# The first cross-attention's context made in the front of the self-attention, four lasting SBUF regions

## What is computed

```python
# 0: decoder block, 16 heads of 16; enc is the context
x = x + causal_attention(ln(x) @ qkv_w + qkv_b) @ proj_w + proj_b
k, v = enc @ k_w + k_b, enc @ v_w + v_b              # "context" of the first chain
x = x + attention(ln(x) @ q_w + q_b, k, v) @ out_w + out_b
x = x + gelu(ln(x) @ mlp1_w + mlp1_b) @ mlp2_w + mlp2_b
# 1: gated state update routed over tokens
tok = ctx @ W_proj + b_proj                            # "context" of the first chain, too
routed = softmax(x @ tok.T / 16) @ tok
x = ln((1 - u) * x + u * tanh(concat(r * ln(x), ln(routed)) @ W_n + b_n))
# 2: self-attention with 16 heads of 64, cross-attention over the context, gated feed-forward
# 3: cross-attention with 8 heads of 256 over the context, then ln
```

## Time and profile before

| | us |
|---|---|
| median of 3 runs | 2376.32 (2376.06 to 2378.35) |
| the profiled execution | 2376.05 |
| its span on the core | 2374.3 |

### The profile page before, as it was taken

The page is one execution under the profiler, slowest core; times in us unless marked ns, Lnnn a source line. Parts: engine busy times, 40 slices in busy tenths (PEclk is TensorE's granted clock), DMA queues, the critical chain, the costliest instruction groups (busy, mean ns, idle before and its releaser), DMA issues. The chain is left out here.

```text
span 2374.3 us, 27271 instructions
## 1 busy us (share of the span) xinstructions
PE 2087.5 (88%) x10510; PEld 1202.8 (51%) x10550; DVE 1119.0 (47%) x2012; ACT 932.2 (39%) x1435; POOL 776.8 (33%) x508
## 2 busy tenths in 40 slices
PE   3789998487979767999999999999998989898987
PEld 1444444275757554433343335334433857676766
DVE  5377662435252435455535554555450143535343
ACT  2246666133323222555545553554455322122211
POOL 3211100013032120566646664666466010202011
PEclk8899999799989887999999999999999989898989
DMA  5822420400000004000000000000000510000000
GB/s 115 131 39 38 51 29 2 113 1 0 1 0 0 1 1 122 1 1 1 1 1 1 1 1 1 1 1 2 1 2 1 161 28 1 9 1 9 0 9 9
DMA packets 48266, 52.77 MB, mean 22 GB/s; under 512 B 14730, under 2 KB 39052, under 8 KB 47732
## 3 DMA queue, kind: packets, MB, share of 16 engines
q1 hardware_dynamic: 48148, 51.17, 10.3%
HBM read 41.31 MB, written 8.80 MB: 21 GB/s over the span
## 5 line engine op out<-in xcount | busy, mean ns | idle before, releaser
L1734 POOL TENSOR_TENSOR total<-total,pr 128x1024 f32<-128x1024 f32 x192 | 464.9, 2421 | 241.9 <-ACT pr L1875 229.0
L1875 ACT ACTIVATE pr<-sc 128x1024 f32<-128x1024 f32 x256 | 259.7, 1021 | 355.6 <-PE sc L1654 355.6
L1755 DVE TENSOR_REDUCE pmax<-ring 128x1 f32<-128x512 f32 x512 | 325.8, 684 | 133.9 <-PE ring L1621 126.9
L1672 PE MATMUL o<-pr,v_pair 128*64 128x512 f32 x1024 | 275.7, 617 | 1.2
L1654 PE MATMUL sc<-q_full,k_full 64*128 64x512 f32 x1024 | 267.1, 591 | 0.0
L522 ACT ACTIVATE probs<-s 128x512 f32<-128x512 f32 (+1 forms) x304 | 163.2, 575 | 102.3 <-PE s L309 55.7
L1621 PE MATMUL ring<-k_round,q_round 64*128 64x512 f32 x512 | 185.0, 598 | 5.2 <-DVE pmax L1755 4.3
L1030 POOL TENSOR_TENSOR c_scores<-c_scores,c_total 128x1024 f32<-128x1024 f32 (+1 forms) x48 | 77.0, 1614 | 338.3 <-DVE c_total L986 338.3
L1621 PEld LDWEIGHTS ring<-k_round,q_round 64*128 64x128 f32 x512 | 74.4, 188 | 155.2 <-DVE pmax L1755 97.2
L394 DVE TENSOR_REDUCE row_max<-s 128x1 f32<-128x640 f32 (+3 forms) x128 | 127.3, 1020 | 47.4 <-PE s L291 47.1
L1672 PEld LDWEIGHTS o<-pr,v_pair 128*64 128x64 f32 x1024 | 51.2, 134 | 144.2 <-issue 142.4
(11 more groups left out here) (286 smaller groups left out, 3421.9 us busy)
## 6 DMA issues: line engine op xcount, KB each, us to landing
qk_dram<-qk_parts SPq DMA_DIRECT2D x32, 192.0 KB, 3.0
q_stack<-qk_dram SPq DMA_DIRECT2D x48, 128.0 KB
k_stack<-qk_dram SPq DMA_DIRECT2D x48, 128.0 KB
x<-in_x SPq DMA_DIRECT2D x4, 512.0 KB, 7.5
mlp_w<-in_L_xattn_mlp_w SPq DMA_DIRECT2D x2, 1024.0 KB, 8.3
wq<-in_L_xattn_Wq SPq DMA_DIRECT2D x2, 1024.0 KB, 6.5
wo<-in_L_xattn_Wo SPq DMA_DIRECT2D x2, 1024.0 KB, 14.9
hT<-in_L_xattn_ff_w SPq DMA_DIRECT2D x1, 2048.0 KB, 19.0
```

What stands on the lines that cost most here:

```text
L1672: ins = te.matmul(o[64 * j:64 * j + 64], v[n % 2][:, kt, 64 * j:64 * j + 64], probs[(U * n + u) % KEPT][:, j], start=kt == 0, stop=kt == T ...
L1734: pool.tensor_tensor(out=total[half][:], in0=other[:], in1=probs[at % KEPT][:], op=ALU.add).then_inc(sums, 1)
L1755: dve.tensor_reduce(part_max[:, j, t, half:half + 1], ring[i % RING][:], AX.X, ALU.max).then_inc(s1_free, 1)
L1875: act.activation(probs[here % KEPT][:], s2[at % 2][:], ACT.Exp).then_inc(s2_free, 1)
```

## The change

- The context work moves into `part_attention0`. Ten loads follow the projection's weights on SyncE. TensorE transposes the context before front unit 10, and multiplies after unit 12 and before `tops(0)`, with four more small matmuls for the values' bias. ScalarE keeps the results (it also scales `q_b` and writes `vcol`, which VectorE did), and `tops(0)` waits for it. GpSimd clears `vcol` behind `v_all`.
- The projection's bias is added to `x` by GpSimd in four pieces between head groups 1 to 4, in place of VectorE's one instruction.
- The 20 small loads of the chain are issued after head group 6 and awaited at the end of `part_attention0`; the five large ones (3.5 MB) are issued in `part_project0` and awaited by TensorE alone, inside the chain's first block.
- `bias0` and `kbd` are made by VectorE in `part_project0`. `part_context0` is gone.
- `ff2_w` of the last chain is loaded at the start of `part_chain2`, and TensorE waits for it at its first use.
- Four SBUF regions last through the program and are used in turn under many names. The first attention's scratch lies in `probs` and `qkv_w`.

```diff
-        raw, inverse = sb("raw", [P, 512]), sb("inverse", [P, 4, 4])
+        inverse = sb("inverse", [P, 4, 4])
...
-        h, hT = e.sa, sb("hT", [P, KC, B * T])
+        h, hT = e.sa, e.hT0
         qkv_w, qkv_b = sb("qkv_w", [P, KC, 3 * C]), sb("qkv_b", [P, 4])
-        rest = [sb(f"qk_rest{i}", [P, 512]) for i in range(RING)]
+        raw = qkv_w[:, 0, 0:512]
+        flat = [t[:].rearrange("p j n -> p (j n)") for t in probs[1:4]]
+        rest = [flat[0][:, 512 * i:512 * i + 512] for i in range(RING)]
         parts = [sb(f"qk_parts{i}", [P, 3, 512], BF16) for i in range(RING)]
+        k_w, v_w, t_w = (flat[2][0:96, 512 * i:512 * i + 512].rearrange("p (k c) -> p k c", k=2) for i in range(3))
+        ctx_rows = flat[1][:, 0:CC]
+        v_brep, t_brep = flat[1][0:S2, 256:512], flat[1][0:S2, 512:768]
+        tri, tri_bf = sb("tri", [P, P]), sb("tri_bf", [P, P], BF16)
+        k_b, t_b, q_b = sb("k_b", [P, KC]), sb("t_b", [P, KC]), sb("q_b", [P, KC])
...
+        CONTEXT, TURNED_AT = 10, 10
...
+            context_loads = [
+                (ctx_rows, lambda r: A["ctx_768"].rearrange("b s c -> (b s) c")),
+                (k_w, lambda r: r("L0_xattn_k_w")), (k_b[:], lambda r: column(A["L0_xattn_k_b"], KC)),
+                (v_w, lambda r: r("L0_xattn_v_w")), (v_brep, lambda r: A["L0_xattn_v_b"].partition_broadcast(S2)),
+                (t_w, lambda r: r("L1_xattn_W_proj")), (t_b[:], lambda r: column(A["L1_xattn_b_proj"], KC)),
+                (t_brep, lambda r: A["L1_xattn_b_proj"].partition_broadcast(S2)),
+                (q_b[:], lambda r: column(A["L0_xattn_q_b"], KC)),
+                (e.mask8[:], lambda r: A["mask_BxS2_bf0"].rearrange("b s -> (b s)").partition_broadcast(P)
+                 .rearrange("p (b s) -> p b s", b=B))]
+            assert len(context_loads) == CONTEXT
...
+            rows96 = lambda n: A[n].rearrange("(k p) c -> p k c", p=96)
+            for dst, src in context_loads:
+                sp.dma_start(dst, src(rows96)).then_inc(ctx_in, 16)
...
+                if n == G - 2:
+                    for dst, src in small:
+                        sp.dma_start(dst, src).then_inc(e.small_in, 16)
+            sp.wait_ge(e.small_in, 16 * len(small))
...
+                    pool.memset(e.vcol[:], 0.0).then_inc(power_set, 1)
...
+                if n <= 4:
+                    if n == 1:
+                        pool.wait_ge(e.proj_in, 48)
+                        pool.wait_ge(h_made, TILES // 2)
+                    pool.wait_ge(rows_cleared, n)
+                    x = e.x[:, 4 * n - 4:4 * n, :]
+                    pool.tensor_tensor(out=x, in0=x, in1=e.proj_brep[:].unsqueeze(1).to_broadcast([P, 4, C]),
+                                       op=ALU.add).then_inc(bias_added, 1)
+                    pool.wait_ge(bias_added, n)
...
+                if i == 0:
+                    te.wait_ge(ctx_kept, 5)
...
+            def context_turned():
+                te.wait_ge(ctx_in, 16 * CONTEXT)
+                for k in range(2):
+                    ins = te.transpose(s1[0][0:96, k * P:(k + 1) * P], ctx_rows[:, 96 * k:96 * k + 96], e.ident[:])
+                ins.then_inc(ctx_made, 1)
+            def context():
+                te.wait_ge(ctx_kept, 1)
...
+                        ins = te.matmul(dst, e.ident[0:S2, 0:S2], v_brep, start=False, stop=True)
...
             for f in range(ALONE):
+                if f == TURNED_AT:
+                    context_turned()
                 front(f)
+            context()
...
+            def context():
+                act.wait_ge(ctx_in, 16 * CONTEXT)
+                act.activation(e.q_bs[:], q_b[:], ACT.Identity, scale=0.25)
+                act.wait_ge(power_set, 5)
+                act.wait_ge(ctx_made, 2)
+                for g in range(KC):
+                    ins = act.activation(e.k_rows[:, g, :], s1[0][:, 512 + g * P:512 + (g + 1) * P], ACT.Identity,
+                                         bias=k_b[:, g:g + 1])
+                ins.then_inc(ctx_kept, 1)
...
+                if f == TURNED_AT:
+                    act.wait_ge(ctx_made, 1)
+                    act.activation(e.ctxT[:], s1[0][0:96, 0:256].rearrange("p (k s) -> p k s", k=2),
+                                   ACT.Identity).then_inc(ctx_kept, 1)
+                if f == ALONE:
+                    context()
...
+                    elif u == 0:
+                        act.wait_ge(low_made, qk_of[NF - 1])
...
+        @block.sync
+        def _(sp):
+            for done, loads in zip(e.chain_in, e.large):
+                for dst, src in loads:
+                    sp.dma_start(dst, src).then_inc(done, 16)
...
-            te.wait_ge(e.proj_in, 48)
...
-                    te.wait_ge(added, u - 2)
+                    te.wait_ge(added, u - 3)
...
-            bias = e.proj_brep[:].unsqueeze(1).to_broadcast([P, TILES, C])
-            dve.tensor_tensor(out=e.x[:], in0=e.x[:], in1=bias, op=ALU.add).then_inc(added, 1)
-            dve.wait_ge(added, 1)
-            for u in range(N):
...
-def part_context0(nc, e, A, later):
...
-            for dst, src in later:
-                sp.dma_start(dst, src).then_inc(later_in, 16)
-            sp.wait_ge(later_in, 16 * len(later))
...
+            for u in range(N):
+                add(u)
+                if u < 2 * B:
+                    b, g = divmod(u, KC)
+                    rep = e.k_rows[:, g, b * S2:(b + 1) * S2].unsqueeze(1).to_broadcast([P, 8, S2])
                     dve.tensor_tensor(out=e.kbd[:, b, g].rearrange("p (h s) -> p h s", s=S2), in0=rep, in1=head_rep,
                                       op=ALU.mult)
...
+    e.large = [[(w.m1, rows("L0_xattn_mlp1_w"))], [(w.m2, rows("L0_xattn_mlp2_w"))],
+               [(w.wu, rows("L1_xattn_W_u")), (w.wr, rows("L1_xattn_W_r")), (w.wn, rows("L1_xattn_W_n"))]]
     cols = {"ln2_g": "L0_xattn_ln2_w", "ln2_b": "L0_xattn_ln2_b", "ln3_g": "L0_xattn_ln3_w", "ln3_b": "L0_xattn_ln3_b",
             "st_g": "L1_xattn_g_state", "st_b": "L1_xattn_beta_state", "in_g": "L1_xattn_g_input",
             "in_b": "L1_xattn_beta_input", "r_b": "L1_xattn_b_r", "l2_g": "L2_xattn_ln1_g", "l2_b": "L2_xattn_ln1_b"}
+    loads = [(e.q_w, rows("L0_xattn_q_w")), (e.o_w[:], rows("L0_xattn_out_w")),
...
+                if first:
+                    te.wait_ge(e.chain_in[0], 16)
...
+                    te.wait_ge(e.chain_in[1], 16)
+                    te.wait_ge(e.chain_in[2], 48)
...
+        w = [e.sa_w0, e.sa_w1] + [[sb(f"sa_w{n}{i}", [P, KC, 256]) for n in "qkv"] for i in range(2, CHUNKS)]
+        wo_w, wo_brep = e.wide, sb("wo_brep", [P, C])
...
+        rden, raw = e.spare, [e.vcol[:].rearrange("p b c d -> p (b c d)"), e.o_w[:].rearrange("p k c -> p (k c)")]
...
+        wqT = e.wide
+        kT, vT = e.kT2, sb("vT2", [P, 8, P])
...
-    w.f1, w.f1b, w.f2 = e.hT, bb("ff1_b", [P, 16]), bb("ff2_w", [P, 8, C])
-    loads = [(w.f1[:], rows("L2_xattn_ff_w1")), (w.f1b[:], column(A["L2_xattn_ff_b1"], 16)),
-             (w.f2[:], rows("L2_xattn_ff_w2"))]
+    w.f1, w.f1b, w.f2 = e.hT, bb("ff1_b", [P, 16]), e.wide
+    loads = [(w.f1, rows("L2_xattn_ff_w1")), (w.f1b[:], column(A["L2_xattn_ff_b1"], 16)),
+             ]
+    e.f2_load = (w.f2, rows("L2_xattn_ff_w2"))
...
+        gate, inner = e.gate, ch.pT
+        result = e.result
...
+            sp.dma_start(*e.f2_load).then_inc(f2_in, 16)
...
+                    te.wait_ge(f2_in, 16)
...
+        first, second, third, fourth = (region(f"region{i}", n) for i, n in enumerate((4096, 8192, 4096, 2048)))
+        e.sa = first[:].rearrange("p (t c) -> p t c", c=C)
+        e.hT = first[:].rearrange("p (k n) -> p k n", k=KC)
+        e.v_all = second[:].rearrange("p (b g t j d) -> p b g t j d", b=B, g=4, t=TB, j=4)
+        e.chain_w0 = views(second, (2048, 2048, 1024, 1024, 1024))
+        q, k, v, o = views(second, (2048,) * 4)
+        e.ctx_w0 = (q.rearrange("p (k c) -> p k c", k=KC), k[0:96].rearrange("p (k c) -> p k c", k=2),
+                    v[0:96].rearrange("p (k c) -> p k c", k=2), o.rearrange("p (k c) -> p k c", c=C))
+        e.gate = [w.rearrange("p (f n) -> p f n", n=256) for w in views(second, (1024, 1024))]
+        tiles = [w.rearrange("p (t c) -> p t c", c=C) for w in views(second[:, 2048:], (512,) * 4)]
+        e.result, e.tail_h = tiles[0:2], tiles[2:4]
+        e.hT0 = third[:].rearrange("p (k n) -> p k n", k=KC)
+        *sa_w0, q_w, biases = views(third, (512,) * 4 + (4 * C + B * 512,))
+        e.sa_w0, e.sa_w1 = ([w.rearrange("p (k c) -> p k c", k=KC) for w in ws]
+                            for ws in (sa_w0, views(third[:, 1536:], (512,) * 3)))
+        e.kT2 = third[:, 512:1536].rearrange("p (k n) -> p k n", n=P)
+        e.spare = views(third[:, 3072:], (512, 512))
+        e.q_w = q_w.rearrange("p (k c) -> p k c", k=KC)
+        e.kbd = fourth[:].rearrange("p (b g n) -> p b g n", b=B, g=KC)
+        e.wide = fourth[:].rearrange("p (k c) -> p k c", c=C)
...
-        part_project0(nc, e)
-        attn.close()
...
```

(4 more changed lines are left out.)

310 lines of the change are left out of this document (112 added, 198 removed).

## The result

The changed kernel takes 2344.72 us (median of 4, 2343.26 to 2346.12), the kernel before in the same comparison 2376.38 us (2376.06 to 2378.35). The ratio is 0.9865, 95% interval 0.9848 to 0.9882. The profiled execution has a span of 2343.2 us against 2374.3, so 31.1 us less. The table sets the two profiles side by side, stage by stage, with marks that both have: TensorE's first transposes, the first trip of score maxima, the starts of the parts. A top trip is the step in which SyncE sends a head group's score maxima to HBM and fetches them back (`tops`).

What follows compares the result with a forecast made beforehand. TensorE was taken as close to fully busy nearly everywhere except the first context, where all engines wait at both ends. 2376.05 - 32.0 + 0.5 = 2344.55 us, median 0.27 above: 2344.8 us; range 2340 to 2351.

Steps and rivals of the forecast that it cites:

- The stage: First context, 418.1 to 450.1 us: deleted, so its whole length on the path goes, -32.0 us.
- `vcol`'s fill: Front: GpSimd's new fill behind `v_all` holds VectorE's first `normed` and TensorE's transposes, +0.5 us, bounds 0 and +0.5.
- Context work in the front: TensorE's 13.8 us of moved matmuls fit its 16.55 us wait for the stack: 0, bounds 0 and +1.0.
- wait cut to 2 or 3 us: Sign in the front: TensorE's stack wait falls from 16.55 us, idle time still ending at 67.5 to 68.5 us.
- Ten loads ahead of SyncE's copies: Front: row copies and mask come up to 3 us later, but nothing needs them sooner: 0.
- GpSimd's adds: First attention: four bias adds of 2.35 us don't stop VectorE: 0, bounds 0 and +9.4 us.
- Small loads: Behind head group 6: twenty issues take at most 20.7 us and fit between SyncE steps 32.4 us apart: 0.
- The rival for slower: Twenty small loads delay group 7's maxima; gain eaten from 64 us of issuing, 2381 us from 69; chance 0.02.
- Large loads: Projection: 3.5 MB at 185 GB/s land in 19 us, TensorE's new waits have 40 us in hand: 0.
- `ff2_w`: Second context: arithmetic bounds it with 3.4 us to spare, so moving the load gives 0; SyncE's end wait goes.
- The clock at the chain's start: Chain's first 42.9 us: TensorE may start warm or its clock rise later: 0, bounds -6.6 and +2 us.
- the rival left with VectorE's share in the way: Chain's first block runs warm: at most 6.6 us, 2338.2; with VectorE about a third, 2342.5; chance 0.10.

Runs made afterwards that it cites:

- Experiment 5: The kernel before, with the chain's five large weights issued last in the context stage and awaited only by TensorE in the chain: 2370.31 us, ratio 0.9977.
- experiment 10: The changed kernel with `vcol` filled in a later gap and unread matmuls keeping TensorE busy in the chain's first block: 2342.57 us, ratio 0.9852.
- experiment 8: The changed kernel with TensorE making the context's values twice in the front, 12 more matmuls: 2343.22 us, ratio 0.9866 to the kernel before.
- experiments 3 and 7: The changed kernel with the projection's bias back on VectorE, 2343.41 us; and with three more adds behind each of GpSimd's four, 2344.55 us.
- experiment 9: The changed kernel with 80 more small loads issued by SyncE behind its 20 behind head group 6: 2378.92 us, ratio 1.001 to the kernel before.
- Experiment 1: The changed kernel with SyncE waiting for all five large transfers at the end of the projection: 2346.19 us, ratio 0.9868 to the kernel before.
- experiment 6: The kernel before, with only the load of `ff2_w` moved from the second context to the start of the last chain: 2376.07 us, ratio 1.0004.

## Why the prediction came out

It said 2344.8 us, and 2344.72 was measured. The main term was read off a stage that stood alone; most of the rest was a list of zeros, and the runs say which of them were zeros for the reason given. That the two agree to 0.1 us is luck: outside the stage the lines of the table run from -0.57 to +0.67 and add up to +1.0 where the sum had +0.5, the front alone has a play of 2.5 us, and the kernel before itself had medians of 2375.84 to 2377.54 us in the comparisons of the experiments. The 32 us aren't luck.

- **The stage, -32.0 us:** right, 32.10 between the two profiles. The split of it was not: "ten microseconds of waiting, eleven of small work, ten of waiting again" reads as if the last ten could be had by dropping the wait. Experiment 5 got 5.4 to 6.2, since SyncE was still issuing for 4 us after the arithmetic had ended. Repeated profiles of this unchanged stage were 0.8 us apart as well.
- **`vcol`'s fill, +0.5:** right: 0.54 us for the fill, 7.45 us for VectorE's first `normed` as one of the two signs had it, transposes 0.46 us later in every kernel with it and not in experiment 10. The Trainium skill, "SBUF — State Buffer", section "Who interferes with whom", has VectorE blocked fully and not slowed; by that rule, the trace agrees (the first `normed` grew from 6.99 to 7.45 us, the others stayed at 0.40). But the landmarks behind it did not move, for a reason that I hadn't in the sum: TensorE's first twelve q and k matmuls took 7.76 us in the profile before and 7.25 in the one after, which is the clock coming back at another moment. (Single matmuls start 0.86 us apart until 33 us in the profile before and until 32.5 us in the one after, and 0.43 us behind. The windows print 1.00 for the whole time up to 40 us, but the trace's first record of the clock is the return to 1.00, at 33.3 and 32.8 us.) Over 14 profiles, from the first transposes to the first stack load it is 25.2 to 25.4 us in eight, whose first record is at 26.7 to 28.1 us, and 27.0 to 27.8 in six, where it is at 32.4 to 33.5, kernels of before and of after in both groups. Beside a play of 2.5 us, 0.46 can be seen in the transposes alone.
- **Context work in the front, 0:** right, but the cover was mis-sized. I took the matmuls at the lower clock, 13.8 us and about 2 us left; they ran in 11.6 us (50.65 to 62.27) at a granted clock of 1.00, and 5.05 us are left. The sign "wait cut to 2 or 3 us" was wrong: it is 5.68. Past the cover (experiment 8) the cost is met by a gain of about the same size, so the upper bound of +1.0 was no bound that mattered.
- **Ten loads ahead of SyncE's copies, 0:** the copies came at 14.99 instead of 14.45 us, and nothing waited for them.
- **GpSimd's adds, 0:** right, and for the reason given (experiments 3 and 7): 28 us more of them changed nothing. The 4.42 us instruction gave nothing when it went.
- **Small loads, 0:** right. They took 11.35 us, against at most 20.7. The rival for slower had the right mechanism and the right point, 32.4 us free, the gain eaten at 64 us of issuing: in experiment 9 some 61 us of it took all but 2 us of the gain in the profile, and all of it by the medians. Only it takes a hundred loads at 0.61 us to get there, not twenty at 3.2.
- **Large loads, 0:** right, but 185 GB/s was the mean of a stage that also waited for its issues. The 3.5 MB landed in 13.8 us, and TensorE had 49 us in hand and not 40. Experiment 1 shows the sign "no wait in the chain" for what it is: none was needed.
- **`ff2_w`, 0:** right (experiment 6). The sign was wrong: SyncE's wait at the stage's end didn't go, it is 3.6 us. In the profile before, the issue of `ff2_w` took 13.3 us; now the small load that took its place in the queue does, and the end of the row is where it was, in the changed kernel:

```profile
1849.81 5.50 SPq L1944 DMA_DIRECT2D region<-in_L_xattn_ff_w  x1
1855.35 0.99 SPq L1944 DMA_DIRECT2D ff_b<-in_L_xattn_ff_b  x1
1856.39 13.01 SPq L1944 DMA_DIRECT2D c_ln_g<-in_L_xattn_ln_g  x1
...
1872.67 0.43 SPq L1944 DMA_DIRECT2D region<-in_L_xattn_ff_b  x1
```

- **The clock at the chain's start, 0, bounds -6.6 and +2:** the chain took 0.67 us more. At the first MLP matmul it was 0.70 behind, at the third block's 0.57 ahead, at the end 0.67 behind again. The level was 1.00 at the start, fell at 421.9 us and came back at 428.7, 10.8 us into the chain instead of 9.9. That isn't a cost of the change: in the ten profiles whose first block is unchanged, the time to the first MLP matmul is 42.77 to 44.17 us, with 42.85, 43.46 and 44.17 in the three that begin at 0.50 and 42.77 to 43.73 in the seven that begin at 1.00. The Trainium skill, "TensorE: Matmul & The Clock Gate", Part 1, says that when the clock comes back differs between runs of one kernel; by that rule, the trace agrees (1.4 us of spread here, 2.5 in the front). Beginning warm was worth nothing that shows: the level fell at 421.9 us, behind an idle 4.27 us and 0.65 us of transposes. The -6.6 was far too wide: with the clock at 1.00 all through (experiment 10) 2.66 us came back, near the third of it that the rival left with VectorE's share in the way. That VectorE holds the rest (32.95 of the 42.9 us busy) is argued, not shown.

What stays open: how much of the 0.33 us in the second attention and 0.13 in the last chain is the same play; no run was made for it.

## What to carry to other kernels

A stage that every engine waits for at both ends is worth its whole length once each of its steps has a gap elsewhere, and each gap should be read for how much it leaves, not only that it holds. Moving the issue of a transfer early pays; dropping the wait for it may pay nothing, and an issue that nobody awaits can itself hold a stage's end. Where TensorE idles a few microseconds in front of dependent small steps, unread matmuls that fill the gap and hardly more kept the clock up and gave about 24 us here; measure their length first, and judge over the whole chain, as one block's gain was taken back by the next.

## What was not expected of the hardware

- The issue of a transfer on SyncE took up to 13 us with 5.5 MB of loads issued in the 9 us ahead of it, and the long issue was once that of a 1 MB load (13.32 us) and once that of a single vector (13.01 us). With the queue near empty it was 0.4 to 0.5 us; in a row of 80 small ones 0.61 us.
- TensorE's clock comes back at different moments for the same work: the same twelve matmuls in the front took 5.39 us in eight profiles and 7.16 to 7.84 us in six. A single profile of this kernel therefore can't tell 2 us in the front from nothing. Between the first and the eighth top trip, where nothing hangs on that return, the two profiles differ by 0.03 us.
- 6.3 us more of TensorE work in a wait with 5 us of room cost nothing that the times could show: the scores behind it then ran at a granted clock of 1.00 instead of 0.50.
